# A fused transformer block with other engine orders, other bank tables, and identity matmuls that may be written into a later unit's bank

## The chip, the core and the metric

One core of a Trainium2 chip. The program is written engine by engine: TensorE (PE) multiplies and writes to PSUM, which has eight banks; VectorE (DVE) and ScalarE (ACT) read the banks; GpSimd (POOL) works on SBUF; SyncE (SP) issues the DMAs. Each engine runs its own list of instructions in order and waits on semaphores for the others. The metric is the time of one execution on the device in microseconds.

## What is computed

Four blocks in a row over 32 sequences of 256 rows and 128 features, all in float32. Each block adds to its input what it makes of the normalised input:

```python
x = L0_attn_x                                             # (32, 256, 128)
x = x + _L0_attn_ref(_layernorm(x), Wq, Wk, Wv, Wu)       # 16 heads of 8, softmax over 256 keys
x = x + _L0_ffn_ref(_layernorm(x), w1, b1, w2, b2)        # relu(x @ w1 + b1) @ w2 + b2, 512 wide
x = x + _L1_attn_ref(_layernorm(x), wq, wk, wv, wo)       # 16 heads, rotary, causal, then @ wo.T
x = x + _L1_ffn_ref(_layernorm(x), wqkv, q_scale, ...)    # two layers, each:
    # shift half of the features by one token; q, k l2-normed, scaled and rotated;
    # softmax in windows of 64 with the window before; x += o @ wo
    # shift, layernorm, h @ w1 + b1; x += (a * gelu(g)) @ w2 + b2
```

## The kernel before

The work is cut into six streams, each of which goes through the 32 sequences in order: ATTN0 (0: first attention and its feed-forward), ATTN1 (1: second attention), LOCAL0 and LOCAL1 (2, 3: the windowed attention of the two layers), FEED0 and FEED1 (4, 5: their feed-forward). A stream is a list of **units** (`stream_units`), numbered within a sequence: ATTN0 has `stats`, `apply`, `turn`, `qkv` 0 and 1, `turn_q`, `turn_k`, `maxes` 0 to 3, `negmax`, `turn_q` with maxima, then `scores` and `mix` four times, and so on to `down0`. A unit has a part on each engine that it needs.

What decides the order is written out: for each engine a string of digits, `FIRST + ROUNDS * TURNS + LAST`, says from which stream the next unit is taken. `TURNS` holds 159 units, one sequence's worth of every stream, each stream being at another sequence; it is repeated `ROUNDS` = 27 times. `FIRST` fills the pipeline and `LAST` empties it. `plan()` reads these strings; it also deals out the PSUM banks that PE's units write, from the strings `FIRST_BANKS`, `BANKS` and `LAST_BANKS`. A unit of PE waits until its banks have been emptied by the engine that reads them (`free`, `taken`, `newest`).

Steps that the prediction follows, with their lines in the profile: PE turns a tile (L1079, L1102, L1217, L1255 to L1257, L1177), projects (`qkv` L1085, `qkv2` L1205), makes ATTN0's `maxes` (L1123; four banks each, two tiles of 256 scores in each) and `scores` (L1146), `mix` (L1168), `project2` (L1278), `up0` (L1190), `down0` (L1198). DVE reduces the maxima (L924), packs them (`negmax`: cast L932, subtract L934), normalises (L892), scales local probabilities (`norm2`, L1017) and rotated q and k (`scale2`, L996), copies a shifted half of the rows for FEED0 and FEED1 (`shift_rows`, L881 and a memset L882). ACT empties turned tiles (L775, L748, L821), takes exponentials (L784, L816). POOL zeroes the upper triangle of ATTN1's probabilities (L683), adds and multiplies for the rotation (L675, L704, L711) and raises to the power -1/2 (`norms2`, L716: 128x16; L664: 128x2).

Ahead of some units PE issues **fillers**, matmuls of the identity with itself (L1058, 128x512 each) into a bank of the unit itself, which its own first matmul overwrites. In before they come from `STEADY_FILLERS`: (4, 3) ahead of `maxes` 1 of ATTN0 and (3, 0) ahead of `shift` of LOCAL0, the first number being how many, the second which of the unit's banks; and from `END_FILLERS` for some units of the first and the last sequences. PE waits for the one bank, then issues them:

```python
for sem, count in newest(free(u)[spare:spare + 1]):
    pe.wait_ge(sem, count)
for _ in range(fillers):
    mm(tile(u, spare)[:].rearrange("p (a k) -> p a k", a=4), ident_r[:], ...)
```

Of the kernel before, what the change touches and what calls it, by code (L numbers as in the profile page):

```python
# [27 lines left out]
def shape_constants():  # L28
# [45 lines left out]
ROUNDS = 27  # L74
# [17 lines left out]
    "vector": (
        "0000000000000000000000000000000000011000000000000111000000111110000000001000000100010000000001111111"
        "1111111111122222200000011122222222222111110000122220000012222200001020220002222200000002222200111111"
        "2411111141111114222222000000111222222222221111100001224422440000401222223313300000332023003302333222"
        "2233333000000022222011111120333311111144333334111311331222200000022113333312333332223225222221111100"
        "001442242245000223"
# [1234 lines left out]
```

## Time and profile before

| | before |
|---|---|
| time, median of 3 runs | 2930.44 us |
| lowest, highest | 2928.8, 2930.98 us |
| the profiled execution, its time | 2930.59 us |
| its span, first to last instruction | 2928.9 us |
| mean granted clock of TensorE | 0.981 |
| instructions | 65080 |

Times in the rows below count from the start of the span. A busy engine is one with an instruction under way. In the rows by slices, each digit is one fortieth of the span, 73.2 us, in tenths; in the clock row, 9 is full speed (2.4 GHz) and a slice at half speed (1.2 GHz) would have 5. In a timeline, consecutive instructions of one form are one row, with the time from the first one's start to the last one's end; idle time ahead of the row stands in square brackets, with what ended it.

### The profile page before, as it was taken

How to read it: one execution, taken by the hardware profiler on the slowest of the kernel's cores; microseconds unless marked ns; L12 is line 12 of the kernel's file. 1: busy time of each engine (PE TensorE's matmuls, PEld its weight loads, DVE VectorE, ACT ScalarE, POOL GpSimd, SP SyncE). 2: the span in 40 equal slices, each digit the busy share in tenths (PEclk: the TensorE clock that was granted, in tenths of full speed). 3: DMA queues.
4: the chain of work that ended last, by engine and by line, in shares of the span. 5: the costliest groups of instructions: out<-in, count | busy, mean ns of one | idle time of the engine just before them, and what ended most of it. 6: DMA issues, size and time to landing. Idle time of an engine off the chain costs nothing.

```text
span 2928.9 us, 65080 instructions
## 1 busy us (share of the span) xinstructions
PE 2649.9 (90%) x24276; PEld 1904.7 (65%) x24276; DVE 2304.0 (79%) x5760; ACT 2127.3 (73%) x5956; POOL 1577.1 (54%) x1749
## 2 busy tenths in 40 slices
PE   4678999999999999999999999999999999999887
PEld 2445666666666666666666666666766666666665
DVE  3457888888888888888888888888888888887763
ACT  2356787778778777777877777777777777777763
POOL 1035565565556556555655655565565555556652
PEclk8789999999999999999999999999999999999998
DMA  2000000000000000000000000000000000000000
GB/s 81 3 3 4 5 5 4 7 7 6 7 7 5 4 7 7 6 7 7 5 4 7 7 6 7 7 5 4 7 7 6 7 7 5 4 7 7 3 6 6
DMA packets 41968, 22.40 MB, mean 8 GB/s; under 512 B 21130, under 2 KB 40884, under 8 KB 41652
## 3 DMA queue, kind: packets, MB, share of 16 engines
q1 hardware_dynamic: 41652, 18.24, 2.3%
q8 instruction: 192, 3.15, 0.4%
q14 instruction: 124, 1.02, 0.1%
HBM read 9.86 MB, written 4.19 MB: 5 GB/s over the span
## 4 chain that ended last, share of the span: by engine, by line
PE 47%; ACT 31%; DVE 14%; POOL 4%; issue 3%; DMA 1%; SPq 0%; POOLq 0%; DVEq 0%; ACTq 0%
ACT probs L784 8%; PE bank L1205 6%; ACT P L816 6%; PE bank L1286 5%; PE bank L1168 4%; DVE negmax L924 4%; PE bank L1217 4%; PE bank L1278 4%; PE bank L1102 3%; ACT rawP L816 3%; PE bank L1146 2%; PE bank L1123 2%; PE bank L1190 2%; PE bank L1243 2%; PE bank L1237 2%
## 5 line engine op out<-in xcount | busy, mean ns | idle before, releaser
L784 ACT ACTIVATE probs<-bank 128x512 f32<-128x512 f32 (+1 forms) x1024 | 478.4, 567 | 193.8 <-PE bank L1146 192.8
L924 DVE TENSOR_REDUCE negmax<-bank 128x2 f32<-128x512 f32 (+1 forms) x896 | 550.1, 680 | 40.2 <-PE bank L1123 38.6
L1205 PE MATMUL bank<-wqkv_sb,hS 128*128 128x512 f32 x768 | 415.1, 625 | 51.4 <-ACT hS L753 29.8
L716 POOL TENSOR_TENSOR rn<-ss_kept,minus_half 128x16 f32<-128x16 f32 x128 | 373.0, 2914 | 6.8 <-DVE ss_kept L987 6.8
L661 POOL TENSOR_TENSOR veps<-moments,eps_tile 128x2 f32<-128x2 f32 x192 | 38.0, 198 | 561.2 <-DVE moments L876 561.2
L683 POOL TENSOR_SCALAR_AFFINE_SELECT probs<-probs 128x256 f32<-128x256 f32 x512 | 210.3, 435 | 208.3 <-ACT probs L784 207.9
L704 POOL TENSOR_TENSOR rawA<-rawA,rope_sb 128x512 f32<-128x512 f32 x128 | 164.9, 1289 | 283.4 <-ACT rawA L803 283.4
L1168 PE MATMUL bank<-probs,V 128*32 128x256 f32 (+1 forms) x4096 | 250.6, 363 | 21.3 <-POOL probs L683 14.4
L704 POOL TENSOR_TENSOR rawB<-rawB,rope_sb 128x512 f32<-128x512 f32 x128 | 179.0, 1399 | 112.0 <-ACT rawB L803 112.0
L973 DVE TENSOR_REDUCE ss<-P 128x8 f32<-128x512 f32 x256 | 174.4, 681 | 77.9 <-ACT P L800 75.8
L1007 DVE TENSOR_REDUCE negmax<-bank 128x2 f32<-128x384 f32 (+1 forms) x384 | 207.0, 595 | 34.2 <-PE bank L1243 33.6
L816 ACT ACTIVATE P<-bank,negmax 128x192 f32<-128x192 f32 x512 | 208.6, 455 | 4.0 <-DVE negmax L1007 1.5
L800 ACT ACTIVATE P<-bank 128x512 f32<-128x512 f32 x256 | 163.4, 638 | 54.1 <-PE bank L1205 51.0
L1286 PE MATMUL bank<-feed_hT,w_sb 128*128 128x256 f32 (+1 forms) x768 | 200.0, 386 | 1.3 <-ACT feed_hT L745 1.3
L1168 PEld LDWEIGHTS bank<-probs,V 128*32 128x32 f32 x4096 | 110.3, 110 | 130.9 <-issue 52.9
L1205 PEld LDWEIGHTS bank<-wqkv_sb,hS 128*128 128x128 f32 x768 | 119.7, 191 | 100.9 <-ACT hS L753 37.3
L816 ACT ACTIVATE rawP<-bank,negmax 128x128 f32<-128x128 f32 x512 | 180.2, 378 | 5.3 <-DVE negmax L1007 4.9
L775 ACT ACTIVATE qT<-bank 128x512 fp32r<-128x512 f32 x256 | 155.8, 685 | 35.5 <-PE bank L1102 35.3
L1286 PEld LDWEIGHTS bank<-feed_hT,w_sb 128*128 128x128 f32 (+1 forms) x768 | 134.2, 179 | 68.0 <-issue 41.8
L711 POOL TENSOR_TENSOR rawB<-rawB,rawP 128x512 f32<-128x512 f32 x128 | 175.1, 1368 | 0.6 <-DVE feed_h L892 0.6
L1102 PE MATMUL bank<-ident_r,QB 128*128 128x128 f32 x1024 | 144.4, 283 | 29.4 <-DVE KB L917 20.6
L1102 PEld LDWEIGHTS bank<-ident_r,QB 128*128 128x128 f32 x1024 | 118.1, 144 | 70.0 <-DVE KB L917 36.8
(140 smaller groups left out, 7156.5 us busy)
## 6 DMA issues: line engine op xcount, KB each, us to landing
xin<-x SPq DMA_DIRECT2D x32, 128.0 KB, 3.1
out<-xout SPq DMA_DIRECT2D x32, 128.0 KB, 1.8
feed_h<-YB SPq DMA_DIRECT2D x64, 63.5 KB
wqkv_sb<-wqkv SPq DMA_DIRECT2D x1, 1536.0 KB
feed_h<-YB SPq DMA_DIRECT2D x64, 0.2 KB
rawQ<-c_masks SPq DMA_DIRECT2D x1, 832.0 KB
w_sb<-w SPq DMA_DIRECT2D x1, 682.0 KB
w_sb<-w SPq DMA_DIRECT2D x2, 256.0 KB, 3.0
```

Of the source, the lines that this page charges most:

```text
L683: nc.gpsimd.affine_select(out=part, in_=part, compare_op=ALU.is_ge, fill=0.0, base=0, pattern=[[0, 2], [1, P]], channel_multiplier=-1)\
L704: nc.gpsimd.tensor_tensor(raw, raw, tab, ALU.mult).then_inc(sig("cos_part", u), 1)
L711: nc.gpsimd.tensor_tensor((q2, k2)[m][:, l, t, :], (q2, k2)[m][:, l, t, :], sines[m][:, l, t, :], ALU.add)\
L716: nc.gpsimd.tensor_tensor(rn[:, l, t].rearrange("p m h -> p (m h)"), ss_kept[:, l, t].rearrange("p m h -> p (m h)"), minus_half[:], ALU.po ...
L784: nc.scalar.activation(dst, src, ACT.Exp, scale=SCALE0 if k == ATTN0 else SCALE1)\
L816: last = nc.scalar.activation(dst, src, ACT.Exp, bias=negmax[:, k, t, hd:hd + 1], accum_out=expsum[:, l, t, hd:hd + 1])
L924: nc.vector.reduce_max(negmax[:, k, t, head:head + 4 * many - 3:4], tile(u, e)[:, :].rearrange("p (h k) -> p h k", h=many), AX.X, negate=T ...
L1007: nc.vector.reduce_max(dst, src, AX.X, negate=True).then_inc(sig("max_done", u), 1)
L1102: last = turn(tile(u)[:, e * SEQ + t * P:e * SEQ + (t + 1) * P], src[:, k, t, 4 * g:4 * g + 4, :].rearrange("p h c -> p (h c)"), ident)
L1168: last = mm(tile(both)[32 * n:32 * n + 32, q0:SEQ], V[:, k, t, 32 * (4 * g + n):32 * (4 * g + n) + 32], part, start=both is u and t == 0, ...
L1205: mm(tile(u)[:], hS[:, l, t * P:(t + 1) * P], wqkv2_sb[:, l, m * INNER:(m + 1) * INNER], start=True, stop=True).then_inc(has_filled(u), 1)
L1286: last = mm(tile(u)[0:n, half * SEQ:(half + 1) * SEQ], w1_2_sb[:, l, half * HID + at:half * HID + at + n], hT[k], start=True, stop=True)
```

## The change

All five order strings and the three bank strings are new, and the boundary between start, rounds and end is drawn elsewhere: 26 rounds for 27, 453 of PE's units ahead of them for 419, 501 behind them for 376. Each engine still does every unit once. The fillers are named by a unit's number, not by its kind, and have a third number: how many, how many units ahead in PE's order the unit stands whose bank they are written into (0 for the unit itself), and which of its banks. In the rounds there are 4 for 7, all ahead of `shift` of LOCAL0, written into a bank of the unit behind it. Before the rounds there are 256 for 60, behind them 185 for 91. The instructions themselves are as before.

```diff
-ROUNDS = 27
+ROUNDS = 26
 FIRST = {
     "tensor": (
-        "0000000000000000000000000000000000000000000000111000010010011110010001000000100000000001110101010111"
+        "0000000000000000000000000000000000000000000000111000011000011110010001000000101110000000001001101101"
...
-STEADY_FILLERS = {(ATTN0, "maxes", 1): (4, 3), (LOCAL0, "shift", 0): (3, 0)}
+STEADY_FILLERS = {(LOCAL0, 0): (4, 1, 0)}
 END_FILLERS = {
-    (0, ATTN0): {("mix", 0): 7, ("mix", 1): 6},
-    (1, ATTN0): {("maxes", 2): 5, ("mix", 0): 4},
-    (0, ATTN1): {("mix", 1): 5},
-    (2, ATTN0): {("mix", 0): 4},
-    (30, LOCAL0): {("shift", 0): 6, ("qkv2", 0): 4, ("scores2", 1): 5},
-    (31, LOCAL0): {("shift", 0): 6, ("qkv2", 0): 4},
-    (30, LOCAL1): {("turn_p", 0): 15},
-    (31, LOCAL1): {("turn_q2", 0): 19},
-    (31, FEED1): {("turn", 0): 27, ("down2", 0): 5},
+    (0, ATTN0): {5: (4, 1, 0), 9: (3, 0, 3), 10: (4, 0, 3), 11: (8, 0, 0), 12: (6, 0, 3), 14: (9, 1, 0), 16: (2, 0, 3), 17: (6, 1, 1), 19: (6, 1, 0), 21: (6, 1, 3), 23: (6, 1, 0), 24: (1, 0, 0), 29: (12, 1, 0), 32: (3, 0, 0)},
+    (0, ATTN1): {5: (5, 0, 0), 9: (2, 0, 0), 13: (5, 0, 0), 18: (2, 1, 3), 20: (3, 1, 3), 22: (1, 1, 3), 25: (3, 0, 0)},
...
+    (31, LOCAL1): {1: (2, 0, 0), 6: (4, 3, 0), 21: (29, 1, 0), 25: (2, 0, 0), 29: (3, 1, 0), 33: (2, 2, 0), 38: (2, 0, 0), 39: (2, 0, 0)},
+    (31, FEED0): {7: (4, 0, 0)},
+    (31, FEED1): {3: (29, 0, 0), 4: (2, 0, 0), 7: (4, 0, 0)},
 }
...
-    for u in orders["tensor"]:
+    for turn, u in enumerate(orders["tensor"]):
+        u.turn = turn
...
-                fillers, spare = STEADY_FILLERS.get((k, u.kind, u.part), (0, 0))
-                if u.sequence > 0 or u.number > 2:
-                    fillers = END_FILLERS.get((u.sequence, k), {}).get((u.kind, u.part), fillers)
+                first = len(FIRST["tensor"])
+                steady = first <= u.turn < first + ROUNDS * len(TURNS["tensor"])
+                table = STEADY_FILLERS if steady else END_FILLERS.get((u.sequence, k), {})
+                fillers, ahead, spare = table.get((k, u.number) if steady else u.number, (0, 0, 0))
                 if fillers:
-                    for sem, count in newest(free(u)[spare:spare + 1]):
+                    later = orders["tensor"][u.turn + ahead]
+                    for sem, count in newest(free(later)[spare:spare + 1]):
                         pe.wait_ge(sem, count)
                     for _ in range(fillers):
-                        mm(tile(u, spare)[:].rearrange("p (a k) -> p a k", a=4), ident_r[:],
+                        mm(tile(later, spare)[:].rearrange("p (a k) -> p a k", a=4), ident_r[:],
```

Three places show what the strings do. In the lists of after, lines of PE lie 29 higher (L1058 is L1087, L1123 is L1152, L1146 is L1175, L1205 is L1234), lines of POOL 27 higher (L716 is L743, L711 is L738, L683 is L710, L675 is L702).

PE in a round, from `maxes` 0 of ATTN0 on. Before:

```order
L1123 MATMUL bank<-kT,qT 128x256 x8
L1146 MATMUL bank<-qT,kT 128x256 x4
L1146 MATMUL bank<-qT,kT 128x128 x4
L1058 MATMUL bank<-ident_r 128x512 x4
L1123 MATMUL bank<-kT,qT 128x256 x8
```

and at the same place after:

```order
L1175 MATMUL bank<-qT,kT 128x256 x4
L1175 MATMUL bank<-qT,kT 128x128 x4
L1234 MATMUL bank<-wqkv_sb,hS 128x512
L1152 MATMUL bank<-kT,qT 128x256 x8
L1284 MATMUL bank<-ident_r,rawP 128x128
L1285 MATMUL bank<-ident_r,P 128x128
L1286 MATMUL bank<-ident_r,P 128x128
L1234 MATMUL bank<-wqkv_sb,hS 128x512
```

Two `qkv2` units of LOCAL1 (L1234) stand where the four fillers stood; in before they come behind `project2`, on either side of a `mix` and a `scores` of ATTN1.

POOL in a round, ahead of the masks of ATTN1's first group of scores. Before:

```order
L716 TENSOR_TENSOR rn<-ss_kept,minus_half 128x16
L696 TENSOR_TENSOR feed_h<-YB,b_2_sb 128x256
L711 TENSOR_TENSOR rawA<-rawA,rawQ 128x512
L661 TENSOR_TENSOR veps<-moments,eps_tile 128x2
L664 TENSOR_TENSOR rstd<-veps,minus_half 128x2
L711 TENSOR_TENSOR rawB<-rawB,rawP 128x512
```

and after:

```order
L688 TENSOR_TENSOR veps<-moments,eps_tile 128x2
L691 TENSOR_TENSOR rstd<-veps,minus_half 128x2
L743 TENSOR_TENSOR rn<-ss_kept,minus_half 128x16
L738 TENSOR_TENSOR rawA<-rawA,rawQ 128x512
L738 TENSOR_TENSOR rawB<-rawB,rawP 128x512
L731 TENSOR_TENSOR rawA<-rawA,rope_sb 128x512
L731 TENSOR_TENSOR rawB<-rawB,rope_sb 128x512
L743 TENSOR_TENSOR rn<-ss_kept,minus_half 128x16
L710 AFFINE_SELECT probs<-probs 128x2x128 x4
L749 TENSOR_TENSOR xout<-XB,YB 128x256
L738 TENSOR_TENSOR rawA<-rawA,rawQ 128x512
L710 AFFINE_SELECT probs<-probs 128x2x128 x4
```

The power of LOCAL1's first tile moved behind ATTN0's statistics, that of the second tile ahead of the first masks (L710), and the last addition (L738 on rawB) ahead of the masks of the third group.

PE at the start of the program, first sequence of ATTN0, from `turn_k` on. Before:

```order
L1102 MATMUL bank<-ident_r,KB 128x128 x8
L1123 MATMUL bank<-kT,qT 128x256 x8
L1058 MATMUL bank<-ident_r 128x512 x4
L1123 MATMUL bank<-kT,qT 128x256 x24
L1102 MATMUL bank<-ident_r,QB 128x128 x8
L1146 MATMUL bank<-qT,kT 128x256 x8
L1058 MATMUL bank<-ident_r 128x512 x7
```

and after:

```order
L1131 MATMUL bank<-ident_r,KB 128x128 x8
L1087 MATMUL bank<-ident_r 128x512 x3
L1152 MATMUL bank<-kT,qT 128x256 x8
L1087 MATMUL bank<-ident_r 128x512 x4
L1152 MATMUL bank<-kT,qT 128x256 x8
L1087 MATMUL bank<-ident_r 128x512 x8
L1152 MATMUL bank<-kT,qT 128x256 x8
L1087 MATMUL bank<-ident_r 128x512 x6
L1152 MATMUL bank<-kT,qT 128x256 x8
L1087 MATMUL bank<-ident_r 128x512 x9
L1131 MATMUL bank<-ident_r,QB 128x128 x8
```

Fillers (L1087) stand ahead of each of the four `maxes` and of `turn_q` with maxima; the work between them is the same.

## Rows read from the trace of the kernel before

**Rows 1.** The page: busy time, the clock by slices, the chain that ended last.

```profile
PE 2649.9 (90%) x24276; PEld 1904.7 (65%) x24276; DVE 2304.0 (79%) x5760; ACT 2127.3 (73%) x5956; POOL 1577.1 (54%) x1749
...
PEclk8789999999999999999999999999999999999998
...
PE 47%; ACT 31%; DVE 14%; POOL 4%; issue 3%; DMA 1%; SPq 0%; POOLq 0%; DVEq 0%; ACTq 0%
```

**Rows 2.** Timeline of PE (start, length, what): one filler group, rounds 1 and 27.

```profile
386.47 1.19 PE L1058 MATMUL bank<-ident_r 128*128 128x512 f32 x4
...
2604.34 1.20 PE L1058 MATMUL bank<-ident_r 128*128 128x512 f32 x4
```

**Rows 3.** Busy time by stretch (PE, PEld, DVE, ACT, POOL, clock): one round.

```profile
1211.70:1297.00 85.30, 80.27 (x757) 58.01 (x756) 71.62 (x180) 66.13 (x188) 49.03 (x54) 1.00 0.02 6
```

**Rows 4.** The same view: sum of the 17 stretches at half clock.

```profile
sum 112.30, PE 89.27 PEld 57.97 DVE 47.47 ACT 40.70 POOL 30.23; mean PE 5.25 PEld 3.41 DVE 2.79 ACT 2.39 POOL 1.78
```

**Rows 5.** Timeline of PE in a round, from ATTN0's maxes to its second turn_q.

```profile
1238.43 0.50 PE L1123 MATMUL bank<-kT,qT 32*128 32x256 f32 x8
...
1239.96 1.20 PE L1058 MATMUL bank<-ident_r 128*128 128x512 f32 x4
1241.25 0.51 PE L1123 MATMUL bank<-kT,qT 32*128 32x256 f32 x8
...
1250.69 1.02 PE L1205 MATMUL bank<-wqkv_sb,hS 128*128 128x512 f32 x2
1251.64 0.86 PE L1168 MATMUL bank<-probs,V 128*32 128x256 f32 x16
...
1252.81 1.12 PE L1205 MATMUL bank<-wqkv_sb,hS 128*128 128x512 f32 x2
1253.77 0.60 PE L1102 MATMUL bank<-ident_r,QB 128*128 128x128 f32 x4
```

**Rows 6.** Timeline of DVE, the same round: negmax of ATTN0.

```profile
1251.23 1.18 DVE L932 CAST QB<-negmax 128x32 fp32r<-128x32 f32 x1
1252.44 0.22 DVE L934 TENSOR_TENSOR QB<-negmax,QB 128x32 fp32r<-128x32 f32 x1
```

**Rows 7.** Timeline of ACT, the same round: turned k of ATTN0, turned q of ATTN1.

```profile
1237.14 1.24 ACT L775 ACTIVATE kT<-bank 128x512 fp32r<-128x512 f32 x2
1238.09 1.27 ACT L775 ACTIVATE qT<-bank 128x512 fp32r<-128x512 f32 x2
```

**Rows 8.** Timeline of DVE, later in the round: the row shift of FEED1.

```profile
1291.72 0.21 DVE L881 COPY feed_h<-YB 128x128 f32<-128x128 f32 x1
1291.89 0.11 DVE L882 MEMSET feed_h<- 1x64 f32 x1
```

**Rows 9.** One line's instructions: shortest, median and longest in ns.

```profile
L932 DVE CAST QB<-negmax x64: 180/192/1181, 32.2 to 2748.0; 128x32 fp32r<-128x32 f32 x64
```

**Rows 10.** Timeline of POOL, the same round.

```profile
1251.08 1.28 POOL L711 TENSOR_TENSOR rawB<-rawB,rawP 128x512 f32<-128x512 f32 x1
...
1276.53 0.73 POOL L675 TENSOR_TENSOR rawC<-rawC 128x256 f32<-128x256 f32 x1 [1.70 <-DVE rawC L910]
1277.21 2.91 POOL L716 TENSOR_TENSOR rn<-ss_kept,minus_half 128x16 f32<-128x16 f32 x1
```

**Rows 11.** Timeline of PE at the end: fillers ahead of FEED1's last turn.

```profile
2907.71 6.39 PE L1058 MATMUL bank<-ident_r 128*128 128x512 f32 x27
```

**Rows 12.** Busy time by stretch: sum of 0 to 340 and 2700 to 2928.9 us.

```profile
sum 568.90, PE 430.05 PEld 297.57 DVE 328.22 ACT 301.15 POOL 214.90; mean PE 215.03 PEld 148.78 DVE 164.11 ACT 150.58 POOL 107.45
```

**Rows 13.** Timeline of PE at the start: fillers, a turn, the first up0.

```profile
36.10 3.01 PE L1058 MATMUL bank<-ident_r 128*128 128x512 f32 x7
...
56.22 0.69 PE L1079 MATMUL bank<-ident_r,probs 128*128 128x128 f32 x2 [3.95 <-DVE probs L892]
57.38 3.78 PE L1190 MATMUL bank<-probs,w_sb 128*128 128x256 f32 x8 [0.47 <-ACT probs L748]
```

**Rows 14.** Timeline of PE in a round: half of an up0 at full clock.

```profile
1305.02 1.03 PE L1190 MATMUL bank<-probs,w_sb 128*128 128x256 f32 x4
```

**Rows 15.** One line's instructions, as in rows 9: scale2 on DVE.

```profile
L996 DVE TENSOR_TENSOR rawA<-rawA,rn x128: 670/693/1752, 186.3 to 2882.3; 128x512 f32<-128x512 f32 x128
```

More of the change, by code:

```diff
@@ L94 @@
[L94 to L97, printed above, removed]
+        "0000000000000000000000000000000000000011000000000111000000111110000000001100000100000000000111111001"
+        "1111111111122222200000011122222222222111111000022220000011222220000020220002222200000002222201111110"
@@ L98 @@
+        "2411111141111114222222000000111222222222221111110000442222440000401222223313333000002023003302333222"
+        "2233333000000022222002111111333341111114333334111311331220000002222113333313333322223225222221111100"
+        "001224442254005040105553322222153333000011111"
     ),
@@ L166 @@
+        "3544445444552222222222223333433333333333333333333333333333335353355353544445445533333333333333333333"
+        "3333333333333355555555"
     ),
@@ L174 @@
+    "6277624315240713510437065427031645136725014603570612704105234735726415312706160247561207534673514076"
+    "4315667021356704215677360432605143762540137526043127503126403271567215047623576127426517051062354653"
+    "2074062107513217450231547210416253405703421572640723045172760463025672561432507602451316470231465726"
+    "4520176527634102746320751425076370641527451630125367421035240143274613470234160253145270263524760135"
+    "21427512357412"
 )
 BANKS = (
-    "4706213754306261730231652014076354635720752361046207154326543217064257406126714502634124362071452361"
@@ new lines @@
+    (0, ATTN1): {5: (5, 0, 0), 9: (2, 0, 0), 13: (5, 0, 0), 18: (2, 1, 3), 20: (3, 1, 3), 22: (1, 1, 3), 25: (3, 0, 0)},
+    (0, LOCAL0): {0: (5, 0, 0), 1: (2, 0, 0), 6: (2, 1, 0), 15: (2, 1, 0)},
+    (1, ATTN0): {2: (9, 0, 0), 5: (4, 1, 0), 9: (3, 0, 2), 10: (2, 0, 1), 11: (10, 1, 3), 12: (4, 0, 3), 14: (9, 4, 0), 16: (2, 0, 1), 19: (9, 1, 0), 24: (5, 2, 3), 29: (10, 0, 0)},
+    (1, ATTN1): {5: (13, 0, 0), 9: (2, 0, 0), 10: (2, 0, 1), 13: (2, 1, 0), 22: (2, 1, 0), 25: (3, 0, 0)},
+    (1, LOCAL0): {0: (5, 0, 0), 1: (2, 0, 0)},
@@ new lines @@
+    (2, ATTN0): {5: (4, 0, 0), 9: (2, 0, 0), 10: (3, 1, 0), 12: (2, 0, 3), 14: (2, 1, 0), 32: (3, 1, 2)},
+    (2, ATTN1): {5: (13, 0, 0), 9: (2, 0, 0)},
+    (2, LOCAL0): {0: (5, 2, 2)},
+    (3, ATTN0): {3: (4, 1, 0), 10: (3, 0, 1), 32: (3, 0, 0)},
+    (4, ATTN0): {3: (4, 0, 0)},
+    (29, LOCAL0): {0: (5, 0, 0), 33: (2, 1, 1)},
+    (29, FEED1): {7: (5, 0, 0)},
+    (30, ATTN1): {18: (3, 1, 3), 23: (1, 0, 0)},
+    (30, LOCAL0): {0: (5, 9, 0), 1: (5, 2, 0), 26: (7, 0, 3)},
+    (30, LOCAL1): {25: (3, 0, 1), 29: (16, 9, 0), 33: (2, 0, 0), 38: (2, 0, 0)},
@@ new lines @@
+    (30, FEED0): {7: (5, 0, 0)},
+    (30, FEED1): {4: (2, 0, 0), 7: (11, 4, 0)},
+    (31, ATTN0): {3: (2, 0, 0)},
+    (31, ATTN1): {5: (2, 0, 0), 18: (3, 1, 1), 23: (1, 0, 0)},
+    (31, LOCAL0): {0: (5, 1, 0), 1: (5, 0, 0), 23: (1, 1, 0), 29: (3, 0, 0), 33: (2, 4, 0), 39: (2, 0, 0)},
+    (31, LOCAL1): {1: (2, 0, 0), 6: (4, 3, 0), 21: (29, 1, 0), 25: (2, 0, 0), 29: (3, 1, 0), 33: (2, 2, 0), 38: (2, 0, 0), 39: (2, 0, 0)},
+    (31, FEED0): {7: (4, 0, 0)},
+    (31, FEED1): {3: (29, 0, 0), 4: (2, 0, 0), 7: (4, 0, 0)},
```

120 lines of the change are left out of this document (62 added, 58 removed).

## Prediction

> **What bounds the kernel now.** The page's first part comes first: PE is busy for 2649.9 of 2928.9 us, DVE for 2304.0, and the chain that ended last is 47% PE, 31% ACT and 14% DVE [rows 1]. So PE leads, but the three hand the work to each other, and what a step is worth has to be read place by place. The second view is the clock row of the page: below full speed in the first nine slices and the last one, full between [rows 1]. That cuts the run into three parts: a start, 27 equal rounds, and an end. The four identity matmuls ahead of a `maxes` unit come once a round: first at 386.47 us, 26 rounds later at 2604.34 [rows 2]; (2604.34 - 386.47)/26 = 85.30 us a round. In one round PE is busy for 80.27 us, DVE for 71.62, ACT for 66.13 and POOL for 49.03 [rows 3]: none is full, PE lacks 5.0 us. The rest, 2928.9 - 27 x 85.30 = 626 us, is start and end. Third, the stretches at half clock, twelve in the start and five in the end: 112.30 us together, with PE busy for 89.27 of them [rows 4].
>
> **What the change leaves alone.** Counted through both PE orders, the last bank-using unit of each sequence of ATTN0 and of ATTN1 has exactly the same units ahead of it in both programs, and in the other streams such a unit moves by at most two or three matmul groups. There are 26 rounds for 27, but the boundary alone was moved (front and end tables are longer). The work, the depth of the pipeline and the table loads of ACT per round stay. Three things are left: swaps inside a round, identity matmuls, and the place of POOL's instructions.
>
> **Term 1, the round.** In the DVE-bound stretch of ATTN0's `maxes`, PE waits: four fillers at 1239.96, and `maxes` 1 only at 1241.25 [rows 5]. Two `qkv2` matmul pairs of LOCAL1 come later, at 1250.69 (1251.64 - 1250.69 = 0.95 us) and 1252.81 (1253.77 - 1252.81 = 0.96 us), and only then `turn_q` with maxima at 1253.77 [rows 5]. The change puts both pairs where the fillers stood. PE is then ready 1.91 us earlier; DVE's maxima are ready at 1252.44 + 0.22 = 1252.66 [rows 6], 1.11 us before 1253.77. I take 1.1: DVE ends last then. What was hidden and could come out: ACT's two evictions of the pairs also move, into idle ACT time in the same stretch, and cost nothing.
>
> Against it, ACT is handed one more `turn_q` copy of ATTN1 ahead of these maxes. Two took 1.27 us with their overlap, after two of kT in 1.24 us from 1237.14 to 1238.38 [rows 7]; two begin 0.95 apart (1238.09 - 1237.14), so one is 0.48, and PE began the maxes at 1238.43, on the heels of that copy [rows 5, 7]. So +0.5. For it, DVE's F1 row copy and memset, 0.21 + 0.11 us [rows 8], leave the unbroken DVE stretch from 1288.99 that ends in ATTN0's normalisation: at most -0.3. Three fillers less per round are priced at nothing: their place had a wait under it.
>
> Sum: -1.1 + 0.5 - 0.3 = -0.9 us a round. New neighbours make waits that no row of before can show; I give 0.2 back, the size of the smaller PE waits of a round, and take **-0.7**. The bounds: -1.7, if the cast below frees DVE as well (1.9 for 1.1), and +0.5, if the copy alone counts. The same swaps stand in start and end, so I count 27 rounds: -0.7 x 27 = **-19 us**.
>
> DVE's cast of these maxima takes 1.18 us [rows 6], while its 64 executions have a median of 192 ns and a maximum of 1181 [rows 9]; POOL's add ran from 1251.08 to 1252.36 beside it [rows 10]. The change puts that add ahead of a set of masks. The Trainium skill, page SBUF — State Buffer, section "SBUF: two separate sides", says that DVE and POOL take a shared port pair exclusively and the loser waits for the whole instruction. By that rule the trace agrees at this place, and the cast would fall to 0.19 us; the end of the maxima would come 1.0 us sooner still.
>
> **Term 2, the clock at both ends.** Start and end hold 60 and 91 fillers now and 256 and 185 after, 290 more. At full clock 27 stand in 6.39 us [rows 11], 0.24 us each: 290 x 0.24 = 70 us. PE's idle time in the first 340 us and the last 228.9 together is 568.9 - 430.05 = 138.9 us [rows 12], so there is room, and most stand where PE waits: twelve go before the turn at 56.22, behind an idle time of 3.95 us [rows 13]. The gain is the work that no longer runs at half clock. Eight `up0` matmuls take 3.78 us at 57.38 [rows 13], against 1.03 for four at full clock [rows 14]. All of it: 89.27/2 = 44.6 us [rows 4] if every PE microsecond at half clock were halved and on the path. Some of it is fillers, some lies beside DVE and ACT, and some of these stretches will stay slow. I take four tenths, about what is left when the fillers and the waits on DVE go off: **-17**, some 13 of it in the start, where three quarters of the slow time lie.
>
> Fillers that don't fit in the wait push the path. Going through the 441 end fillers place by place, at 0.213 us each (94 us) against the idle time at the same unit in the trace of before, 85 us fit and 9 don't. Some of the 9 are absorbed downstream: **+4**. At half clock one takes 3.01/7 = 0.43 us [rows 13], and then 55 us would not fit: the bound from the other side.
>
> **Sum.** Against the profiled execution's own 2930.6 us (span 2928.9 and 1.7 around it; the median of the runs is 2930.44, the same): 2930.6 - 19 - 17 + 4 = **2899 us**.
>
> [...]
>
> **Rivals.**
> (a) *The round stays as it is.* The maxima are ready sooner, but the chain behind them (ACT's exponentials of ATTN1, masks, mix, copy) sets the round, and the ACT copy takes back the rest. For it: ACT carries 31% of the chain. Against: ACT's exponentials there queue behind one of the very evictions that move. Round 85.3, ends -13: 2918 us. Chance 0.17.
> (b) *Fillers run at half clock and stand on the path.* The clock needs the very activity that the fillers are to make; fillers there took 0.43 us each and the clock row stayed low in the first slices [rows 1, 13]. With half of the 55 us that don't fit and little clock gained, the ends become about 20 us longer: 2930.6 - 19 + 20 = 2932 us. Chance 0.07. Against: places with four to twelve in a row have waits of that length.
> (c) *Slower: POOL's power instruction meets DVE.* `norms2` on POOL takes 2.91 us [rows 10]. It now stands directly behind ATTN0's statistics, when DVE does `norm2` and `scale2`, and ahead of ATTN1's masks and rotation, which PE and ACT wait for. In before, `scale2` has a median of 0.69 us and a maximum of 1.75 [rows 15]: a meeting costs up to 1.06 us. DVE has little slack before the maxes; from there on each hit goes into the round. The rotation began at 1276.53 and the power behind it at 1277.21; with the two exchanged, it is late once the power starts after 1276.53 - 2.91 = 1273.62 [rows 10]. One hit and 0.7 us of lateness, less the 0.7 of term 1: +1.1 a round, 27 x 1.1 = 30, less 13 at the ends: 2948 us. Chance 0.14. Against: POOL idles for 36 us of a round [rows 3], so most neighbours have room.
> That the change does less than it says is excluded by the orders; the fillers are in them.
>
> **How the numbers follow.** The forecast has 0.62. The low end takes the round at -1.1 (-30) and the ends at -30: 2871. The high end leaves (c) out for the most part and holds (a) and (b): 2932. Within 0.2%, some 6 us, a measurement of this kernel can't be told from no change. Faster by more: the forecast and nearly all of (a), 0.77. Within: (b) and a rest, 0.10. Slower: 0.13.
>
> **What would show it.** Round: the four fillers that remain come every 84.6 us; 85.3 speaks for (a), more for (c). Term 1: no idle time at the second `maxes`, `turn_q` with maxima right behind its cast, the cast at 0.19 us. Term 2: half-clock stretches of 40 to 70 us in all instead of 112, and `up0` of the first pass in some 2 us. (c): `norm2` or `scale2` over 1 us beside the power, POOL as the releaser of PE or ACT. I would be wrong in kind if the round were longer, or if the clock row of the first slices didn't rise.

## The result and the profile after

The changed kernel takes 2880.0 us against 2930.24 us in the same session: ratio 0.9828, 95% interval 0.9813 to 0.9844, some 50 us faster. One of its four executions, at 3439.7 us and a granted clock of 0.712 where the others had 0.997, is left out. The forecast was 2899 with a range of 2871 to 2932: right in sign and held by the range, but 19 us short. The profiled execution has a span of 2878.8 us, 50.1 less than before.

Its page, for [rows 1] (busy time, clock by slices, chain that ended last):

```profile
PE 2665.7 (93%) x24481; PEld 1924.5 (67%) x24481; DVE 2257.9 (78%) x5760; ACT 2121.7 (74%) x5956; POOL 1593.6 (55%) x1749
...
PEclk9999999999999999999999999999999999999999
...
PE 45%; ACT 36%; DVE 9%; POOL 6%; issue 4%; DMA 0%; SPq 0%; POOLq 0%; ACTq 0%; DVEq 0%
```

Every slice of the clock row has a 9 now, the first ones too. DVE is busy for 46 us less with the same 5760 instructions, and its share of the chain falls from 14 to 9%. Where did the 50 us go? PE's timeline (start, length, what) at one unit that both kernels have, ATTN0's turn, in sequence 4 and in sequence 31, of before:

```profile
289.63 0.38 PE L1079 MATMUL bank<-ident_r,probs 128*128 128x128 f32 x2
...
2594.28 0.38 PE L1079 MATMUL bank<-ident_r,probs 128*128 128x128 f32 x2
```

and of after:

```profile
269.35 0.44 PE L1108 MATMUL bank<-ident_r,probs 128*128 128x128 f32 x2 [0.39 <-DVE probs L919]
...
2547.15 0.38 PE L1108 MATMUL bank<-ident_r,probs 128*128 128x128 f32 x2
```

Up to the first row 20.3 us are gained. The 27 sequences between take (2594.28 - 289.63)/27 = 85.36 us before and (2547.15 - 269.35)/27 = 84.36 us after: 1.0 each, 26.9 us in all. What follows takes 334.6 before and 331.7 after: 2.9. The sum is 50.1. One round of after by engine (stretch, PE, PEld, DVE, ACT, POOL, clock), for [rows 3]:

```profile
1198.00:1282.30 84.30, 79.51 (x755) 57.82 (x754) 69.91 (x180) 66.00 (x188) 49.68 (x55) 1.00 0.02 6
```

The same view, the sum of the four stretches at half clock that are left, for [rows 4]:

```profile
sum 18.20, PE 15.41 PEld 10.83 DVE 7.23 ACT 4.57 POOL 1.95; mean PE 3.85 PEld 2.71 DVE 1.81 ACT 1.14 POOL 0.49
```

Half-clock time fell from 112.30 to 18.20 us, PE's busy time in it from 89.27 to 15.41. In a round DVE is busy for 1.71 us less, and 27 times that is its 46 us. PE's timeline of after from ATTN0's first `maxes` to the second `turn_q`, for [rows 5]:

```profile
1206.77 0.51 PE L1152 MATMUL bank<-kT,qT 32*128 32x256 f32 x8
...
1208.05 1.13 PE L1234 MATMUL bank<-wqkv_sb,hS 128*128 128x512 f32 x2 [0.23 <-DVE negmax L951]
1209.34 0.51 PE L1152 MATMUL bank<-kT,qT 32*128 32x256 f32 x8 [0.16 <-DVE negmax L951]
...
1219.43 0.86 PE L1197 MATMUL bank<-probs,V 128*32 128x256 f32 x16 [0.26 <-POOL probs L710]
1220.22 0.45 PE L1175 MATMUL bank<-qT,kT 32*128 32x256 f32 x8
1220.60 0.66 PE L1131 MATMUL bank<-ident_r,QB 128*128 128x128 f32 x4
```

DVE's cast and subtraction in the same round, for [rows 6]:

```profile
1219.55 0.19 DVE L959 CAST QB<-negmax 128x32 fp32r<-128x32 f32 x1
1219.78 0.22 DVE L961 TENSOR_TENSOR QB<-negmax,QB 128x32 fp32r<-128x32 f32 x1
```

POOL's addition and masks around them, for [rows 10]:

```profile
1215.72 1.28 POOL L738 TENSOR_TENSOR rawB<-rawB,rawP 128x512 f32<-128x512 f32 x1
1217.73 1.55 POOL L710 TENSOR_SCALAR_AFFINE_SELECT probs<-probs 128x256 f32<-128x256 f32 x4 [0.73 <-ACT probs L811]
```

ATTN0's turn of this round is at 1198.03, and at 1229.89 in the round of [rows 5]. From there the first `maxes` comes 8.74 us behind it instead of 8.54 (+0.20), and the second `turn_q` after 22.57 instead of 23.88 (-1.31). The cast takes 0.19 us instead of 1.18, because POOL's addition is over before it starts. DVE is done at 1220.00, 0.60 us before PE turns: a mix group that waited 0.26 us for POOL's masks is what ends last.

PE's timeline at the start of after: twelve identities, the first turn of the feed-forward and its `up0`, for [rows 13]:

```profile
50.07 3.00 PE L1087 MATMUL bank<-ident_r 128*128 128x512 f32 x12
54.27 0.44 PE L1108 MATMUL bank<-ident_r,probs 128*128 128x128 f32 x2 [1.20 <-DVE probs L919]
55.18 1.99 PE L1219 MATMUL bank<-probs,w_sb 128*128 128x256 f32 x8 [0.47 <-ACT probs L775]
```

An identity takes 0.25 us here where it took 0.43, `up0` 1.99 where it took 3.78, and 1.20 us of the old idle time of 3.95 remain.

### The profile page after: what moved, and what is told of

Read it like the earlier page. It is cut to its first block, busy times and chain, and to the rows that moved or that the text cites. A ratio compares the mean times of both kernels' runs of the same rounds, so it can differ in the third digit from the quotient of the medians.

```text
span 2878.8 us, 65513 instructions
## 1 busy us (share of the span) xinstructions
PE 2665.7 (93%) x24481; PEld 1924.5 (67%) x24481; DVE 2257.9 (78%) x5760; ACT 2121.7 (74%) x5956; POOL 1593.6 (55%) x1749
## 4 chain that ended last, share of the span: by engine, by line
PE 45%; ACT 36%; DVE 9%; POOL 6%; issue 4%; DMA 0%; SPq 0%; POOLq 0%; ACTq 0%; DVEq 0%
ACT probs L811 8%; ACT P L843 7%; PE bank L1197 5%; PE bank L1234 5%; PE bank L1315 5%; PE bank L1246 4%; PE bank L1131 4%; DVE negmax L951 3%; ACT rawP L843 3%; ACT P L827 3%; PE bank L1152 3%; POOL probs L710 3%; PE bank L1175 2%; PE bank L1272 2%; PE bank L1266 2%
## 5 line engine op out<-in xcount | busy, mean ns | idle before, releaser
L1234 PE MATMUL bank<-wqkv_sb,hS 128*128 128x512 f32 x768 | 394.8, 611 | 13.3 <-DVE negmax L951 6.5
L743 POOL TENSOR_TENSOR rn<-ss_kept,minus_half 128x16 f32<-128x16 f32 x128 | 371.8, 2905 | 58.4 <-DVE ss_kept L1014 56.8
L731 POOL TENSOR_TENSOR rawA<-rawA,rope_sb 128x512 f32<-128x512 f32 x128 | 190.4, 1488 | 243.7 <-ACT rawA L830 243.7
L710 POOL TENSOR_SCALAR_AFFINE_SELECT probs<-probs 128x256 f32<-128x256 f32 x512 | 197.4, 408 | 156.6 <-ACT probs L811 156.3
L1315 PE MATMUL bank<-feed_hT,w_sb 128*128 128x256 f32 (+1 forms) x768 | 190.7, 384 | 0.7 <-ACT feed_hT L772 0.6
L1234 PEld LDWEIGHTS bank<-wqkv_sb,hS 128*128 128x128 f32 x768 | 125.5, 189 | 85.2 <-issue 40.3
L738 POOL TENSOR_TENSOR rawA<-rawA,rawQ 128x512 f32<-128x512 f32 x128 | 176.8, 1381 | 0.0
L1087 PE MATMUL bank<-ident_r 128*128 128x512 f32 x545 | 163.6, 427 | 6.4 <-DVE rope_sb L875 6.2
L738 POOL TENSOR_TENSOR rawB<-rawB,rawP 128x512 f32<-128x512 f32 x128 | 163.4, 1277 | 0.0
```

What stands on the lines that cost most here:

```text
L710: nc.gpsimd.affine_select(out=part, in_=part, compare_op=ALU.is_ge, fill=0.0, base=0, pattern=[[0, 2], [1, P]], channel_multiplier=-1)\
L731: nc.gpsimd.tensor_tensor(raw, raw, tab, ALU.mult).then_inc(sig("cos_part", u), 1)
L738: nc.gpsimd.tensor_tensor((q2, k2)[m][:, l, t, :], (q2, k2)[m][:, l, t, :], sines[m][:, l, t, :], ALU.add)\
L743: nc.gpsimd.tensor_tensor(rn[:, l, t].rearrange("p m h -> p (m h)"), ss_kept[:, l, t].rearrange("p m h -> p (m h)"), minus_half[:], ALU.po ...
L1234: mm(tile(u)[:], hS[:, l, t * P:(t + 1) * P], wqkv2_sb[:, l, m * INNER:(m + 1) * INNER], start=True, stop=True).then_inc(has_filled(u), 1)
L1315: last = mm(tile(u)[0:n, half * SEQ:(half + 1) * SEQ], w1_2_sb[:, l, half * HID + at:half * HID + at + n], hT[k], start=True, stop=True)
```

## The experiments

Start is the time of ATTN0's turn of sequence 4; round is the mean of the 27 sequences to the turn of sequence 31; rest is what follows; half clock is given for these three parts. All in us, from the traces; the time is the median of the runs (in before, of each session's). A half-clock stretch that outlasts the span is counted whole, so after has 20 us here for 18.2 within its span.

| run | time | ratio to before, 95% | start | round | rest | half clock |
|---|---|---|---|---|---|---|
| before | 2928.3 to 2931.0 | 1 | 289.6 | 85.36 | 334.6 | 82, 3, 29 |
| after | 2880.0 | 0.9828 (0.9813 to 0.9844) | 269.4 | 84.36 | 331.7 | 14, 0, 6 |
| a_nofill | 2914.5 | 0.9952 (0.9933 to 0.9972) | 293.3 | 84.36 | 341.2 | 130, 0, 46 |
| a_oldfill | 2920.4 | 0.9967 (0.9956 to 0.9978) | 294.9 | 84.39 | 345.7 | 113, 0, 35 |
| b_newfill | 2940.3 | 1.0038 (1.0024 to 1.0051) | 294.5 | 85.36 | 339.3 | 48, 3, 12 |
| a_ownbank | 2896.8 | 0.9889 (0.9875 to 0.9904) | 274.3 | 84.40 | 341.4 | 7, 0, 14 |
| a_double | 2926.2 | 0.9983 (0.9973 to 0.9992) | 295.6 | 84.43 | 349.1 | 10, 0, 3 |
| a_qkv2_back | 2962.8 | 1.0109 (1.0076 to 1.0143) | 267.6 | 87.43 | 331.4 | 10, 109, 7 |
| a_qkv2_fill4 | 2943.7 | 1.0048 (1.0033 to 1.0063) | 267.3 | 86.72 | 332.7 | 10, 0, 10 |
| a_nosteady | 2905.2 | 0.9909 (0.9892 to 0.9925) | 267.0 | 85.39 | 333.1 | 10, 85, 9 |
| b_no_maxfill | 2929.3 | 0.9997 (0.9988 to 1.0006) | 291.1 | 85.29 | 330.8 | 96, 0, 15 |
| b_add_early | 2931.2 | 1.0009 (0.9997 to 1.0020) | 290.7 | 85.36 | 335.1 | 61, 0, 29 |
| a_add_late | 2892.3 | 0.9867 (0.9852 to 0.9882) | 267.1 | 84.80 | 333.1 | 10, 0, 10 |
| a_shift_back | 2910.6 | 0.9932 (0.9917 to 0.9947) | 267.8 | 85.54 | 330.5 | 10, 0, 3 |

Starts and rests differ by up to 4 us between runs with the same tables there (267.0 to 269.4; 330.5 to 333.1 and, with the tables of before, 330.8 to 335.1), along with where single half-clock stretches fall. The rounds agree within 0.07.

**The ends without their identities (a_nofill).**

```diff
-END_FILLERS = { ... }
+END_FILLERS = {}
```

> The changed kernel without any filler before and behind the rounds (441 matmuls of the identity less; the 4 in each round stay). Clock theory: the half-clock stretches come back, over 90 us in all instead of 17, the start becomes 15 to 22 us longer, the round stays at 84.3 us, the time is 2898 to 2906 us. Order theory (the new start is faster because its orders are better): the half-clock stretches come back but cost under 6 us, 2881 to 2886 us.

Measured: 2914.5 us, 34.5 above the changed kernel, more than the clock theory had asked for. The rounds don't move (84.36). The start is 23.9 us longer, the rest 9.5. So without any identities the new orders of the start are 3.7 us slower than those of before with their 60, and all of the gain of the start hangs on the identities. What the orders of before would take without theirs was not run. Its clock row in the page:

```profile
PEclk7688999999999999999999999999999999999998
```

and PE's timeline at half clock in it:

```profile
48.55 1.94 PE L1173 MATMUL bank<-probs,V 128*32 128x256 f32 x16 [2.24 <-ACT probs L787]
...
60.70 0.69 PE L1084 MATMUL bank<-ident_r,probs 128*128 128x128 f32 x2 [3.74 <-DVE probs L895]
61.86 3.73 PE L1195 MATMUL bank<-probs,w_sb 128*128 128x256 f32 x8 [0.47 <-ACT probs L751]
```

PE waits 2.24 us and then mixes for 1.94 us; in the changed kernel the same mix took 1.07 us. 33.3 us of span for 156 us more at half clock: 0.21 us for each.

**The old identities on the new orders (a_oldfill).**

```diff
-    table = STEADY_FILLERS if steady else END_FILLERS.get((u.sequence, k), {})
-    fillers, ahead, spare = table.get((k, u.number) if steady else u.number, (0, 0, 0))
+    fillers, ahead, spare = STEADY_FILLERS.get((k, u.number), (0, 0, 0)) if steady else (0, 0, 0)
+    if not steady:
+        fillers = END_FILLERS.get((u.sequence, k), {}).get((u.kind, u.part), 0)
```

> The changed kernel's orders and banks with the end identities of the kernel before: its table of 122 by kind and part, each cluster into its own unit's bank, in place of 441. The rounds are as in the changed kernel. Theory (the ends gain by the clock that the identities hold, the orders there give little): the rounds keep their 26 us, half-clock time comes back to some 110 us as before; by the run without end identities (176 us at half clock, 34 us longer than the changed kernel with 20 us) that is 0.22 us for each us at half clock, so 2880 + 20 = 2900 us (2895 to 2906). Rival (the orders at the start and the end carry the gain there): 2880 to 2888 us.

Measured: 2920.4 us. The rounds keep their gain; start and rest are 25.5 and 14.0 us longer, longer even than with no identities at all. The expected 2900 was 20 too low: it priced the half-clock time alone. 122 identities at places that were chosen for other orders hold the clock little (148 us at half for 176 with none), and the run is 5.9 us slower than with none. (The kernel before issues 151 outside its rounds; the 29 that its table for the rounds adds there are not in this run.)

**The new counts on the old orders (b_newfill).** 402 identities in all at the ends, at the same units as in the changed kernel, each cluster into its own unit's first bank; clusters at units without a bank fall away.

```diff
-    (0, ATTN0): {("mix", 0): 7, ("mix", 1): 6},
+    (0, ATTN0): {5: 4, 9: 3, 10: 4, 11: 8, 12: 6, 14: 9, 16: 2, 17: 6, 19: 6, 21: 6, 23: 6, 24: 1, 29: 12, 32: 3},
...
-                if fillers:
-                    for sem, count in newest(free(u)[spare:spare + 1]):
+                if fillers and u.uses:
+                    later = u
+                    for sem, count in newest(free(later)[spare:spare + 1]):
```

> The kernel before, its orders and banks untouched, with the changed kernel's numbers of fillers before and behind the rounds (230 and 179, where a unit has a bank of its own; written into that unit's first bank). Clock theory: half-clock stretches of under 40 us instead of 112, round 85.3 us as before, 14 to 22 us faster: 2908 to 2916 us. Order theory: 2925 us or more. If they stand on the path: over 2932 us.

Measured: 2940.3 us, 10 above before, though the granted clock rose from 0.981 to 0.990 and half-clock time fell to 63 us. Start +4.9, rest +4.7. A better clock alone doesn't make the ends shorter.

**The banks (a_ownbank).**

```diff
+                if not steady and ahead and u.uses:
+                    ahead, spare = 0, 0
                 if fillers:
                     later = orders["tensor"][u.turn + ahead]
```

> The changed kernel with one thing undone: 25 of the 33 clusters of identity multiplications at the two ends that are written to a bank of a later unit go into the first bank of their own unit again (the other 8 stand at units that use no bank, and stay). Counts and orders are as in the changed kernel. Theory (a cluster into its own unit's bank starts only when that bank is free, so it stands between the wait and the unit, on the path; the run that put the same counts into the own banks of the kernel before ended 10 us above that kernel although its granted clock rose from 0.981 to 0.990): 2884 to 2890 us. Rival (the bank that a cluster goes to doesn't matter, only that PE is kept at work): 2880 us, within 2. Rival (the 10 us of that run came from counts that fit other orders): 2880 too.

Measured: 2896.8 us, +16.8 at the same clock (0.997), where 4 to 10 were expected; the rival of no effect is out. The table has 38 clusters with a later unit's bank, 30 of them at units with a bank of their own (the expectation counts 33 and 25); these 30 moved, each to its unit's first bank. One place in PE's timeline, ten identities at `maxes` 2 of ATTN0, in the changed kernel:

```profile
80.46 2.56 PE L1087 MATMUL bank<-ident_r 128*128 128x512 f32 x10
83.61 0.51 PE L1152 MATMUL bank<-kT,qT 32*128 32x256 f32 x8 [0.59 <-DVE negmax L951]
```

and in this run:

```profile
82.58 0.51 PE L1154 MATMUL bank<-kT,qT 32*128 32x256 f32 x8
84.97 2.56 PE L1089 MATMUL bank<-ident_r 128*128 128x512 f32 x10 [1.89 <-DVE negmax L951]
87.47 0.51 PE L1154 MATMUL bank<-kT,qT 32*128 32x256 f32 x8
```

Written into the later unit's bank, the ten run at once and PE still has 0.59 us left to wait. Written into the own bank, they wait 1.89 us for that bank first, run for 2.56 us, and only then comes the unit, which could have started where they did. The cluster lies behind the wait instead of in it. In the rest this takes all of the gain (341.4 against 341.2 with no identities), in the start 4.9 of 23.9 us.

**Twice as many (a_double).** Each count in the table of the ends doubled, 882 for 441:

```diff
-    (0, ATTN0): {5: (4, 1, 0), 9: (3, 0, 3), ...
+    (0, ATTN0): {5: (8, 1, 0), 9: (6, 0, 3), ...
```

> The changed kernel with the count of each of the 94 clusters of end identities doubled: 882 instead of 441, the rounds untouched. It prices the identities that don't fit in their waits. 441 more at 0.213 us are 94 us. If none of it were covered: 2974 us. If the clusters only fill half of their waits: 2880 us or, with the last 20 us of half clock gone, 2876. Theory (each cluster is about as long as its wait, but the path takes back a part at the next wait of another engine): half of it comes out, some 2925 us (2905 to 2945), at a granted clock of 0.998 or more.

Measured: 2926.2 us, as expected: 45.4 us of span for 94 us of identities, 0.48 of each comes out, at a clock of 0.998. PE's timeline at the start:

```profile
57.18 5.72 PE L1087 MATMUL bank<-ident_r 128*128 128x512 f32 x24
62.74 0.38 PE L1108 MATMUL bank<-ident_r,probs 128*128 128x128 f32 x2
```

The 24 ahead of the turn leave no idle time, where twelve left 1.20 us.

**The two `qkv2` pairs back behind `project2` (a_qkv2_back).**

```diff
-        "0002532213230000332250130232201120113231301330303313110311313301120232231120330122133322332435201111"
+        "0002532213230000332250102220112011231013333330303313110311313301120232231120330122133322332435201111"
```

(PE's string of the rounds. The same move is made in ACT's string of the rounds, and the banks of the rounds are dealt to fit; start and end are untouched.)

> The changed kernel with the two qkv2 pairs of LOCAL1 (parts 2 and 5) back behind project2 and behind the last scores in the 26 rounds, on PE and on ACT, with four banks redealt for it; nothing put in their old place. Swap theory: the second turn_q of ATTN0 comes 1.0 to 1.3 us later, the round is 85.2 to 85.5 us, the time 2903 to 2911 us. Rival (the round is shorter for other swaps, this one is hidden): round under 84.6 us, 2880 to 2888 us.

Measured: 2962.8 us, 83 more instead of 27. Two things in one, which the trace takes apart. In the rounds there are 19 stretches at half clock, 109 us; once the rounds have settled, those without one last 86.1 to 86.4 us; the mean is 87.43. PE's timeline at one of the falls:

```profile
710.29 0.45 PE L1175 MATMUL bank<-qT,kT 32*128 32x256 f32 x8
712.26 0.80 PE L1152 MATMUL bank<-kT,qT 32*128 32x256 f32 x8 [1.52 <-DVE negmax L951]
```

and the stretch behind it by engine:

```profile
712.30:722.50 10.20, 9.67 (x81) 6.28 (x85) 6.73 (x12) 3.05 (x8) 6.30 (x12) 0.50 0.01 2
```

At the place where the pairs stand in the changed kernel, PE waits 1.52 us for DVE's maxima, and from 712.3 on it runs at half clock for 10.2 us, with work to do for 9.67 of them.

**The same with four identities in the gap (a_qkv2_fill4).**

```diff
-STEADY_FILLERS = {(LOCAL0, 0): (4, 1, 0)}
+STEADY_FILLERS = {(LOCAL0, 0): (4, 1, 0), (ATTN0, 10): (4, 0, 3)}
```

> The run with the two LOCAL1 qkv2 pairs behind the maxes again (2962.8 us), and in addition the four identities of the kernel before ahead of ATTN0's maxes 1 in every round, into the fourth bank of that unit. That run lost 1.9 us in a round whose granted clock stayed full (86.1 against 84.25) and 1.3 us more in the mean of all rounds, with 19 stretches at half clock in them, 109 us. Theory (the pairs, like the four identities, are what keeps PE at work while it would wait for DVE's maxima; the swap itself costs 1.9 us in the round and the falling clock the rest): no half clock in the rounds, 2880 + 27 x 1.9 = 2931 us (2926 to 2938). Rival (the clock falls in the rounds for another reason, in the stretch where the pairs are missing no more): stays at 2955 to 2965. Rival (my prediction's own price of the swap, 1.0 us in the round): 2907.

Measured: 2943.7 us; no half clock in the rounds, which last 86.72 us, all alike. The clock part of the theory holds. It is 12.7 us above its 2931: the four are not free here, 0.6 us a round against the 86.1 of a clean round without them. So the swap is worth 2.36 us a round with them, 1.8 without. Where it comes from, in PE's timeline:

```profile
1242.26 1.02 PE L1234 MATMUL bank<-wqkv_sb,hS 128*128 128x512 f32 x2
1243.22 0.86 PE L1197 MATMUL bank<-probs,V 128*32 128x256 f32 x16
...
1244.38 1.13 PE L1234 MATMUL bank<-wqkv_sb,hS 128*128 128x512 f32 x2
1245.35 0.60 PE L1131 MATMUL bank<-ident_r,QB 128*128 128x128 f32 x4
```

and in DVE's:

```profile
1243.03 0.22 DVE L961 TENSOR_TENSOR QB<-negmax,QB 128x32 fp32r<-128x32 f32 x1
```

DVE is done at 1243.25, and PE turns 2.10 us later, because the pairs stand before the turn. In before the same pairs cost 1.11 us there, because DVE itself was late: its cast took a microsecond longer.

**The identities left in the round (a_nosteady).**

```diff
-STEADY_FILLERS = {(LOCAL0, 0): (4, 1, 0)}
+STEADY_FILLERS = {}
```

> The changed kernel without the four identities that each round still holds, ahead of LOCAL0's shift (one cluster of 1.20 us a round); the ends keep theirs. Theory (as in the kernel before, where the run without its four ahead of the maxes changed neither the time nor the clock: the place has a wait under it, and the rest of the round keeps PE at work): 2880 us, within 3, no half clock in the rounds. Rival (they are all that keeps the clock up there, as the qkv2 pairs were in the run that moved them back, 109 us at half clock in the rounds): 2880 + 27 x 1.3 = 2915 us (2900 to 2925). Rival (a part of the cluster stands on the path, at most 0.9 us of it): down to 2860, which would beat both kernels.

Measured: 2905.2 us. The first rival is right: 25 stretches of 3.4 us at half clock in the rounds, and in nearly every round at the same place. PE's timeline there in the changed kernel:

```profile
1231.78 1.20 PE L1087 MATMUL bank<-ident_r 128*128 128x512 f32 x4
1233.49 0.41 PE L1108 MATMUL bank<-ident_r,YB 128*128 128x128 f32 x2 [0.51 <-ACT P L843]
```

in this run:

```profile
1242.71 0.41 PE L1108 MATMUL bank<-ident_r,YB 128*128 128x128 f32 x2 [1.65 <-ACT P L843]
1243.42 0.80 PE L1175 MATMUL bank<-qT,kT 32*128 32x256 f32 x8 [0.30 <-ACT P L843]
1244.15 2.08 PE L1234 MATMUL bank<-wqkv_sb,hS 128*128 128x512 f32 x2
```

and this run's stretch at half clock by engine:

```profile
1243.40:1246.80 3.40, 3.38 (x14) 2.02 (x15) 3.10 (x7) 3.15 (x8) 0.60 (x1) 0.50 0.00 0
```

The four identities (1.20 us) stood in a wait for ACT and hid nothing else. Without them PE waits 1.65 us until 1242.71, the clock falls at 1243.4, the `qkv2` pairs take 2.08 us instead of 1.12, and a round 1.03 us more. The one round between without a fall lasts 84.6 us.

**The same for the kernel before (b_no_maxfill).**

```diff
-STEADY_FILLERS = {(ATTN0, "maxes", 1): (4, 3), (LOCAL0, "shift", 0): (3, 0)}
+STEADY_FILLERS = {(LOCAL0, "shift", 0): (3, 0)}
```

> The kernel before without the four identities ahead of ATTN0's maxes 1 in each round (the three at the shift stay). My prediction priced them at nothing: 2930 us, within 2, clock as before (0.981). Rival, from the run with the pairs moved back (no identities and no pairs in the maxes' wait, 109 us at half clock in the rounds): the clock falls in the rounds here too, and each round gets 1.3 us longer in the mean, 2930 + 27 x 1.3 = 2965 us (2945 to 2975).

Measured: 2929.3 us, no half clock in the rounds, 85.29. My price of nothing was right, the rival wrong: the clock stays up, with PE's idle time at that place as its timeline shows it:

```profile
1240.91 0.50 PE L1123 MATMUL bank<-kT,qT 32*128 32x256 f32 x8 [1.38 <-ACT probs L784]
```

**POOL's additions, both ways (b_add_early, a_add_late).** LOCAL1's last additions ahead of ATTN1's masks in the kernel before, and the fourth one behind them again in the changed kernel (POOL's string of the rounds each time):

```diff
-        "0222030002435003353513555323012333323201032213131120323011313433222120141031302031231101402244012122"
+        "0222030002435003353513555323012333323201032213133112023031113433222120141031302031231101402244012122"
```

```diff
-        "0333333333233310153133131011431040110311311310312341253234304021204302111203024222222310000220320330"
+        "0333333333233310153131133011431040110311311310312341253234304021204302111203024222222310000220320330"
```

> The kernel before with two additions of LOCAL1 on POOL (add2 2 and 3) each one group of ATTN1's masks earlier in the rounds; nothing else. Port theory: DVE's cast of ATTN0's maxima falls from 1.18 to 0.19 us. By my reading PE reaches turn_q 1.1 us after the maxima in this kernel, so the round stays at 85.3 and the time at 2928 to 2932 us. Rival (the cast itself is on the path of the round): round 84.3 to 84.8 us, 2903 to 2917 us. If the cast stays at 1.18 us, POOL's addition isn't its cause.

> The changed kernel with one move on POOL undone: LOCAL1's fourth addition (1.28 us) stands behind the masks of ATTN1's second score group again, as before, and so beside DVE's cast of ATTN0's maxima. Expected in the trace: the cast 1.18 us instead of 0.19 in a round. Theory (the ratio of chip times follows DVE from there): in the changed kernel DVE's subtraction behind the cast ends at 1220.00 and the first turn_q with maxima runs at 1220.60, behind a mix group, so 0.6 of the 1.0 us is covered and 0.4 comes out: 2880 + 27 x 0.4 = 2891 us. Rival (the mix group, released by POOL's masks, is what the turn waits for, and it comes no later with the masks ahead of the addition): 2880 us, within 3. Rival (nothing covers it): 2880 + 27 = 2907.

Measured in before: 2931.2 us, no change, with the cast down to 0.19 us in DVE's timeline:

```profile
1251.64 0.19 DVE L932 CAST QB<-negmax 128x32 fp32r<-128x32 f32 x1
```

Measured in after: 2892.3 us, 0.44 us a round, which is the 0.4 of the theory. DVE's cast in the timeline:

```profile
1221.94 1.03 DVE L959 CAST QB<-negmax 128x32 fp32r<-128x32 f32 x1
```

POOL's addition:

```profile
1221.64 1.28 POOL L738 TENSOR_TENSOR rawB<-rawB,rawP 128x512 f32<-128x512 f32 x1
```

and PE's turn:

```profile
1223.28 0.66 PE L1131 MATMUL bank<-ident_r,QB 128*128 128x128 f32 x4 [0.22 <-DVE QB L961]
```

The cast ends at 1222.97, 0.05 us behind the addition's end at 1222.92; now PE does wait for DVE. The same microsecond is worth nothing in before, where the pairs stand in front of the turn, and 0.44 in after.

**The row copy of FEED1 (a_shift_back).** It stands between the first two `maxes` of ATTN1 again (DVE's string of the rounds):

```diff
-        "21222052211100211023222445405052220401052353020311131050131"
+        "21222022111002151023222445405052220401052353020311131050131"
```

> The changed kernel with one move on DVE undone: FEED1's row copy and memset (0.21 + 0.11 us) stand between the first and the second maxes of ATTN1 again, in the unbroken DVE stretch. My prediction's term: 0.3 us a round, 2880 + 27 x 0.3 = 2888 us. Rival (DVE's delay is caught up before anyone waits for it): 2880 us, within 3.

Measured: 2910.6 us, 1.18 us a round for two instructions of 0.21 and 0.11. DVE's timeline there:

```profile
1269.07 1.25 DVE L908 COPY feed_h<-YB 128x128 f32<-128x128 f32 x1
1270.28 0.11 DVE L909 MEMSET feed_h<- 1x64 f32 x1
```

POOL's:

```profile
1268.98 1.27 POOL L738 TENSOR_TENSOR rawA<-rawA,rawQ 128x512 f32<-128x512 f32 x1
```

and PE's, a little later:

```profile
1273.11 0.44 PE L1206 MATMUL bank<-ident_r,rawC 128*128 128x128 f32 x2 [0.89 <-DVE rawC L966]
```

At this place the copy runs into an addition of POOL and takes 1.25 us instead of 0.21 [rows 8]; PE waits 0.89 us for what DVE does next.

No run beat the changed kernel.

## Why the prediction was right, and where it was off

**The frame** (a start, 27 equal rounds, an end) held: every run's time is the sum of these three, and each part could be read by itself.

**Term 1, the round.** Forecast -0.7, measured -1.0, so -27 for -19. The mechanism was right: the pairs fill the wait in the maxima's stretch and no longer stand before the turn. Its parts: the first `maxes` comes 0.20 us late, not 0.5 (the ACT copy, mis-sized). The turn comes 1.31 sooner with that included, so the pairs gave 1.5 where I had 1.1. The step that failed is the one that left DVE's cast out of the value and put it only into the bound: the move of POOL's addition goes with the swap, and undone by itself it costs 0.44. 1.1 + 0.4 is the 1.5. For the row copy I had -0.3: the lead in the round grows there from 1.24 to 1.56 us. The undo costs 1.18, but mostly for a meeting with POOL that exists only in the new order, so it doesn't size this term. Behind it 0.6 us are given back by the next turn, where I had 0.2. That nothing hangs on three fillers less was right for before.

What the undoings cost doesn't add up to what was gained: 2.36, 1.18 and 0.44 are 4.0 us a round, the gain 1.0. With the pairs back and four identities the round lasts 86.72, 1.36 longer than before's. So the new order without the swap is worse than the old one; that the rest of it was laid around the swap is a reading that no run shows. Which of the other moves in ACT's and DVE's strings carries how much was not tried.

**Term 2, the ends.** Forecast -17 + 4 = -13, measured -20.3 - 2.9 = -23.2. Two sizes were off. I expected 40 to 70 us to stay at half clock; 18 did. PE's busy time at half clock fell by 73.9 us, half of which is 36.9, and 23.2 came out net: six tenths, where I had taken four tenths of the whole less 4. My cap of 44.6 held. The second: the 9 us that don't fit. No run measures them alone, since dropping them changes the clock, but of the next 94 us 0.48 came out. The split between start and end was off too, 20 to 3 for 13 to 4 before the fillers' cost.

And the cause was told too simply. I put the gain to the clock. The runs on the tables show more: new orders with no identities, new orders with the old ones, and old orders with the new counts have starts of 293.3, 294.9 and 294.5 us, all slower than before's 289.6. New orders with the new counts in the own banks have 274.3, and with the later banks 269.4. The identities pay where they lie in a wait. The bank decides this for a part of them: 4.9 of the 23.9 us that they give in the start, and all 9.5 of the rest. I had treated the third number of the table as a detail; it is worth 16.8 us.

**Rivals.** (a), round unchanged: out, 84.36. (b), identities on the path: out for the change, since clock and waits held, but real beyond it (a_double, 0.48 of each). (c), POOL's power meets DVE: out, and with it its price. The power now does stand beside `norm2`. POOL's and DVE's timelines in after:

```profile
1195.57 2.90 POOL L743 TENSOR_TENSOR rn<-ss_kept,minus_half 128x16 f32<-128x16 f32 x1
...
1197.55 0.69 DVE L1044 TENSOR_TENSOR rawP<-rawP,recip 128x512 f32<-128x512 f32 x1
```

`norm2` starts 0.92 us before the power's end and takes the 0.69 us that it takes anywhere (median 693 ns). 28 executions start beside the power like this one, and none takes more than a few ns longer. The long executions of `scale2` (63 over 1 us in before, 39 in after) lie beside POOL's additions and multiplications, none of them beside the power. So the step from the 1752 ns of [rows 15] to a price for the power was wrong. In a_shift_back such an addition does it to a copy, at 1.04 us a hit.

**POOL beside DVE, and the clock.** Cast and copy last until POOL's addition ends (1222.97 against 1222.92; 1270.32 against 1270.25). That is what the Trainium skill, page SBUF — State Buffer, section "SBUF: two separate sides", says of the shared port pair. The trace agrees for the additions, and it belonged in the sum, at 0.4 of its 1.0 us. It doesn't agree for the power: by that rule `norm2`, with both inputs in SBUF, would have waited 0.92 us for it, and it waited for nothing. Of the clock: without the identities at its ends the kernel's span is 33.3 us longer, 1.2%, at a granted clock of 0.970, and without the four of the round it takes 25.2 us more.

## What to carry to other kernels

When work moves into a wait, price the turn that it used to delay together with whatever else ends there: here PE, DVE and POOL each held the same turn, and one microsecond of DVE was worth 0 us with the pairs in front of it and 0.44 without. A matmul that is there only to keep PE busy must be able to start when the wait starts, so write it into a bank that is free by then, and count it: too few and the clock falls, twice as many and half of the surplus comes out. Undoing one move in an order that was fitted as a whole gives that move's price in the new order, not its share of the gain.

## What was not expected of the hardware

The clock fell behind one short wait in a stretch where PE was busy for 79.7 of 85.3 us: 1.65 us idle, then 3.4 us at half clock, in 25 rounds at the same place, for 1.03 us a round. Another place with 1.38 us idle, in the other kernel, had no such effect. And two DVE instructions of 0.32 us together took 1.36 in another place, because POOL had an addition under way, and the round got 1.18 us longer. POOL's longest instruction, the power of 2.9 us, held up none: of the 543 DVE instructions that start under it in after, with 0.3 us of it or more to come, none lasts 0.04 us over its usual time.
